# Third context attention: the filter's spectrum computed inside the self-attention in front of it

## The reference

```python
# self-attention of layer 2: two causal softmax attentions with 16 heads of 8, and their difference
q1, k1, q2, k2 = (x @ W for W in (Wq1, Wk1, Wq2, Wk2));  v = x @ Wv      # v: 16 heads of 16
a1, a2 = softmax(causal(q1 k1^T * scale)), softmax(causal(q2 k2^T * scale))
y = normalise_heads((a1 - lam * a2) @ v) * const;  x = x + y @ Wc

# context attention of layer 2: x -> top 32 of 1601 places per head (4 heads), then a long filter
dt = exp(log_dt);  dtA = dt * (A_re + 1j * A_im)            # 128 channels x 64 states
dC = (C_re + 1j * C_im) * (exp(dtA) - 1) / A
K  = 2 * einsum('dn,dnl->dl', dC, exp(dtA[:, :, None] * arange(256))).real
Kf = rfft(K, n=512)                                         # the filter's spectrum
y  = irfft(rfft(x, n=512) * Kf)[:256] + x * D_skip
```

## Time and profile before

| | us |
|---|---|
| median of 3 runs | 4265.91 |
| profiled execution, its own time | 4270.48 |
| span of the profiled execution, first to last instruction | 4268.6 |
| PE, DVE, ACT, POOL busy | 3312.7, 2984.5, 1868.6, 352.4 |
| `linear_columns`, second time (2503.7 to 2518.7) | 15.0 |
| first `self_attention` (2420.1 to 2503.7) | 83.6 |
| second `self_attention` (2518.7 to 2601.3) | 82.6 |
| first stage of `filter_spectrum` (2635.9 to 2701.2) | 65.3 |
| second stage of `filter_spectrum` (2701.2 to 2717.7) | 16.5 |

### The profile page before, as it was taken

The page is one execution under the profiler, slowest core; times in us unless marked ns, Lnnn a source line. Parts: engine busy times, 40 slices in busy tenths (PEclk is TensorE's granted clock), DMA queues, the critical chain, the costliest instruction groups (busy, mean ns, idle before and its releaser), DMA issues. The chain is left out here.

```text
span 4268.6 us, 58517 instructions
## 1 busy us (share of the span) xinstructions
PE 3312.7 (78%) x23817; PEld 1723.8 (40%) x23826; DVE 2984.5 (70%) x4070; ACT 1868.6 (44%) x2158; POOL 352.4 (8%) x150
## 2 busy tenths in 40 slices
PE   5799999999999965777776883466654669477579
PEld 3433333333333324344434652223222347344357
DVE  4577777777777776699996446699998444546642
ACT  2365565555555542344442233344443236245233
POOL 0000000000000000100000000044442000000000
PEclk9899999999999978799997997656567789688789
DMA  2000000000000000100002001000000100010010
GB/s 83 9 15 8 8 16 8 8 8 16 8 8 10 6 7 7 26 15 9 9 1 94 30 2 48 1 0 0 0 0 0 41 23 18 9 40 1 1 41 6
DMA packets 21598, 68.43 MB, mean 16 GB/s; under 512 B 5201, under 2 KB 5713, under 8 KB 20434
## 3 DMA queue, kind: packets, MB, share of 16 engines
q1 hardware_dynamic: 21330, 64.69, 5.1%
HBM read 49.07 MB, written 0.52 MB: 12 GB/s over the span
## 5 line engine op out<-in xcount | busy, mean ns | idle before, releaser
L1194 PE MATMUL banks<-L0x_ring,L0x_context_rows 128*101 128x512 f32 x1600 | 734.7, 602 | 4.0 <-ACT L0x_ring L1242 4.0
L1253 ACT COPY L0x_ring<-banks 128x1024 f32<-128x1024 f32 (+1 forms) x416 | 387.1, 982 | 536.4 <-PE banks L1182 536.4
L1182 PE MATMUL banks<-L0x_q_thirds,L0x_context_thirds 32*128 32x512 f32 x4800 | 596.2, 608 | 10.3 <-DVE L0x_q_thirds L1359 5.3
L1284 DVE TENSOR_TENSOR L0x_ring<-L0x_ring,L0x_greatest 128x2048 f32<-128x2048 f32 (+1 forms) x208 | 469.9, 2268 | 10.8 <-ACT L0x_ring L1253 9.4
L1300 DVE TENSOR_TENSOR L0x_maxima<-L0x_maxima,L0x_ring 128x1024 f32<-128x1024 f32 (+1 forms) x288 | 322.8, 1162 | 202.8 <-ACT L0x_ring L1253 202.7
L1194 PEld LDWEIGHTS banks<-L0x_ring,L0x_context_rows 128*101 128x101 f32 x1600 | 253.8, 167 | 456.0 <-issue 449.0
L1242 ACT ACTIVATE L0x_ring<-L0x_ring 128x2048 f32<-128x2048 f32 (+1 forms) x208 | 386.4, 1858 | 16.6 <-DVE L0x_ring L1284 16.2
L1182 PEld LDWEIGHTS banks<-L0x_q_thirds,L0x_context_thirds 32*128 32x128 f32 x4800 | 238.1, 186 | 348.5 <-issue 308.2
L1745 ACT ACTIVATE L1x_probs<-banks 128x2048 f32<-128x2048 f32 (+1 forms) x112 | 196.5, 1755 | 252.1 <-PE banks L1679 210.2
L1804 DVE TENSOR_REDUCE L1x_maxima<-banks 128x3 f32<-128x1203 f32 (+1 forms) x176 | 241.4, 1373 | 31.1 <-PE banks L1637 31.1
L1827 DVE SCALAR_TENSOR_TENSOR L1x_probs<-L1x_probs,L1x_floor 128x1024 f32<-128x1024 f32 (+1 forms) x208 | 252.1, 1216 | 11.3 <-ACT L1x_probs L1745 11.1
(11 more groups left out here) (954 smaller groups left out, 5227.2 us busy)
## 6 DMA issues: line engine op xcount, KB each, us to landing
L0x_q_thirds<-L0x_q_context SPq DMA_DIRECT2D x180, 64.0 KB, 2.0
L1f_expert_weights<-in_L1f_experts SPq DMA_DIRECT2D x16, 512.0 KB, 9.7
L2f_expert_weights<-in_L2f_experts SPq DMA_DIRECT2D x8, 512.0 KB, 6.0
L3a_expert_weights<-in_L3a_experts SPq DMA_DIRECT2D x8, 512.0 KB, 5.8
L3f_expert_weights<-in_L3f_experts SPq DMA_DIRECT2D x8, 512.0 KB, 6.5
L1x_k<-L1x_k_rows SPq DMA_DIRECT2D x64, 50.0 KB
L0x_context_thirds<-in_context_thirds SPq DMA_DIRECT2D x1, 2496.0 KB, 14.4
L1x_context<-in_context SPq DMA_DIRECT2D x4, 600.4 KB, 4.5
```

The source lines that it names most:

```text
L1182: mm = pe.matmul(k.ps[:, score_bank(s) + i, :], thirds[group_rows(i), slot, t, :], q_thirds[group_rows(i), u // 2 % 2, t, :], start=t == 0 ...
L1194: mm = pe.matmul(k.ps[0:CW, bank, :], rows1[0:height(j), j, :], ring[0:height(j), s % RING, i, :], start=s == FIRST[u] and i == 0, stop=s ...
L1253: act.copy(ring[0:r, s % RING, 2 * p:2 * p + len(pair), :], k.ps[0:r, bank:bank + len(pair), :]).then_inc(copied, 1)
L1284: dve.tensor_tensor(o, o, greatest[:, u % 2, None, :].broadcast_to([P, len(js), 512]), ALU.subtract).then_inc(shifted, 1)
```

## The change

The first stage of `filter_spectrum` is gone. Its work is spread over four places of layer 2's self-attention, in classes whose methods `linear_columns` and `self_attention` call (`beside`):

- `SpectrumRates`, in the first `linear_columns`: GpSimd computes `dt` and the rates, 29 instructions (12 two-input products, 14 with a scalar, on 128x128, and a memset and two iotas of 16).
- `SpectrumAngles`, in the first `self_attention`: GpSimd makes the multiples of the angle (2 products of 128x2048, with both inputs broadcast) and reduces two 128x128 angles (20 small instructions). DVE reduces the two 128x2048 angles, one or two instructions after `reduce(u+1)` in units 2 to 11. ACT takes all sines after its last unit.
- `SpectrumProducts`, in the second `self_attention`: GpSimd does 47 small instructions and 7 of 128x2048; ACT an exponential of 128x128 in unit 0, one of 128x2048 in unit 3 and one after the last unit; DVE a copy by mask and a reciprocal of 128x128 in unit 7.
- The loads of the spectrum's tables and of the context are issued in the last stage of the self-attention. The two masks are loaded in the stage that was the second of `filter_spectrum`, and ACT widens the context mask there, after its copies.

The working tiles lie where the context and the rows of the context attention lie later, and `best_places` keeps its exponentials where the tables were.

```diff
@@ self_attention
                     act.copy(yT[...], k.ps[:, 4:4 + n, spare]).then_inc(copied, 1)
+                    if beside:
+                        beside.scalar(act, u)
+                if beside:
+                    beside.after(act)
...
+                other = beside.vector(dve) if beside else iter(())
                 reduce(0)
                 for u in range(len(units)):
                     shift(u)
                     if u + 1 < len(units):
                         reduce(u + 1)
+                    next(other, None)
@@ new: the angles on DVE (SpectrumAngles.vector: two units nothing, then this twice)
+def turn_angle_by_turns(step, dve, angle, work, turns, radians, done):
     step(dve.tensor_scalar(work, angle, 1.0 / (2 * float(np.pi)), turns, ALU.mult, ALU.add))
+    step.start(dve.tensor_scalar(work, work, MAGIC, MAGIC, ALU.add, ALU.subtract))
+    yield
+    for c in RANGE:                                    # three constants
+        step.settle()
+        step.start(dve.scalar_tensor_tensor(out=angle, in0=work, scalar=-c, in1=angle, op0=ALU.mult, op1=ALU.add))
+        yield
+    step.settle()
+    step(dve.tensor_scalar(angle, angle, radians, 3.1415925, ALU.add, ALU.min))
+    dve.tensor_scalar(angle, angle, -3.1415925, None, ALU.max).then_inc(done, 1)
+    yield
@@ SpectrumAngles.after, on ACT behind the last unit
+        act.wait_ge(self.bent, 2)
+        act.activation(s2, s2, ACT.Sin).then_inc(self.sined, 1)
+        act.activation(x1, x1, ACT.Sin).then_inc(self.sined, 1)
+        act.wait_ge(self.turned, 1)
+        act.activation(a.high_part, a.high_part, ACT.Sin).then_inc(self.sined, 1)
+        act.wait_ge(self.turned, 2)
+        act.activation(a.low_part, a.sines, ACT.Abs).then_inc(self.sined, 1)
+        act.activation(a.sines, a.sines, ACT.Sin).then_inc(self.sined, 1)
+        act.wait_ge(self.sined, 5)
+        act.activation(a.low_part, a.low_part, ACT.Sin, scale=-1.0, bias=a.quarter).then_inc(self.sined, 1)
@@ SpectrumProducts.gpsimd, from the wait for DVE's unit 7 to the end
+        pool.wait_ge(self.chosen, 2)
...
+        step(pool.tensor_tensor(a.low_part, a.low_part, across(cA), ALU.mult))
+        step(pool.tensor_tensor(a.sines, a.sines, across(cB), ALU.mult))
+        step(pool.tensor_tensor(a.low_part, a.low_part, a.sines, ALU.add))
+        pool.wait_ge(self.exped, 2)
+        step(pool.tensor_tensor(a.low_part, a.low_part, a.decay, ALU.mult))
+        pool.tensor_tensor(a.decay, across(rate), along(a.sixteens), ALU.mult).then_inc(self.rated, 1)
+        pool.wait_ge(self.exped, 3)
+        step(pool.tensor_tensor(a.high_part, a.high_part, a.decay, ALU.mult))
@@ SpectrumProducts.after, on ACT behind the last unit
+        act.wait_ge(self.rated, 2)
+        act.activation(self.a.decay, self.a.decay, ACT.Exp).then_inc(self.exped, 1)
```

More of the change, by code:

```diff
@@ L387, in add_to_residual, with self_attention @@
     return write
-def self_attention(k, ctx_name, qT, kT, v, y, heads, dv, causal=True):
+def self_attention(k, ctx_name, qT, kT, v, y, heads, dv, causal=True, beside=None):
     groups = heads // 4
@@ L3729, in filter_spectrum @@
-def filter_spectrum(k, w, spectrum, c_all, hidden, mask, tiles):
-    full = [P, P, LOW]
-    with ExitStack() as ctx:
-        tables = k.sb("L2s_tables", [P, 2, HIGH // 4, FREQ], ctx=ctx)
-        small = k.sb("L2s_small", [P, 14, P], ctx=ctx)
-        angle, work, ev, U, V = (k.sb("L2s_" + n, full, ctx=ctx) for n in ("angle", "work", "e", "U", "V"))
-        t1, t2 = (tiles[:, 2 * i:2 * i + 2].rearrange("p a t n -> p (a t n)").rearrange("p (n l) -> p n l", l=LOW) for i in range(2))
-        power = k.sb("L2s_two_to_n", [P, P], I32, ctx=ctx)
+RANGE = (6.28125, 0.0019350051879882812, 2 * float(np.pi) - 6.28125 - 0.0019350051879882812)
@@ new lines, in across, with along, __init__, begin @@
+def across(row):
+    return row[:, :, None].broadcast_to([P, P, LOW])
+def along(row):
+    return row[:, None, :].broadcast_to([P, P, LOW])
+class SpectrumRates:
+    def __init__(self, a):
+        self.a = a
+    def begin(self, signal):
+        self.own = signal()
+    def gpsimd(self, pool):
+        a, w = self.a, self.a.w
+        dt, rate, th, em1, s2, nr, ni, wr, wi, mag, cA, cB, x1, x2, inv = a.small
+        pool.wait_ge(a.weights_here, 32)
+        step = Steps(pool, self.own)
+        step.start(pool.memset(a.quarter, float(np.pi / 2)))
+        step.start(pool.iota(a.ones, [[1, LOW]], base=0, channel_multiplier=0, allow_small_or_imprecise_dtypes=True))
+        step(pool.iota(a.sixteens, [[LOW, HIGH]], base=0, channel_multiplier=0, allow_small_or_imprecise_dtypes=True))
+        exponential_apart(step, pool, w["log_dt"], dt, mag, em1, a.power)
+        step.start(pool.tensor_tensor(th, dt, w["A_im"], ALU.mult))
+        step(pool.tensor_tensor(rate, dt, w["A_re"], ALU.mult))
@@ new lines, with __init__, begin, gpsimd @@
+class SpectrumAngles:
+    def __init__(self, a):
+        self.a = a
+    def begin(self, signal):
+        self.own, self.multiplied, self.by_dve, self.bent, self.turned, self.sined = (signal() for _ in range(6))
+    def gpsimd(self, pool):
+        a = self.a
+        dt, rate, th, em1, s2, nr, ni, wr, wi, mag, cA, cB, x1, x2, inv = a.small
+        step = Steps(pool, self.own)
+        pool.tensor_tensor(a.high_part, across(th), along(a.sixteens), ALU.mult).then_inc(self.multiplied, 1)
+        pool.tensor_tensor(a.sines, across(th), along(a.ones), ALU.mult).then_inc(self.multiplied, 1)
+        step(pool.tensor_scalar(s2, th, 0.5, None, ALU.mult))
+        turn_angle_apart(step, pool, s2, mag, em1).then_inc(self.bent, 1)
+        step(pool.tensor_copy(x1, th))
+        turn_angle_apart(step, pool, x1, mag, em1).then_inc(self.bent, 1)
+    def vector(self, dve):
+        a = self.a
+        step = Steps(dve, self.by_dve)
+        yield
+        yield
+        dve.wait_ge(self.multiplied, 1)
+        yield from turn_angle_by_turns(step, dve, a.high_part, a.decay, a.w["turns"], a.w["radians"], self.turned)
+        dve.wait_ge(self.multiplied, 2)
+        yield from turn_angle_by_turns(step, dve, a.sines, a.decay, 0.0, 0.0, self.turned)
+    def scalar(self, act, u):
+        pass
+    def after(self, act):
+        a = self.a
+        s2, x1 = a.small[4], a.small[12]
+        act.wait_ge(self.bent, 2)
[8 more added lines that the diff above has]
+        act.activation(a.low_part, a.low_part, ACT.Sin, scale=-1.0, bias=a.quarter).then_inc(self.sined, 1)
@@ L3742, in filter_spectrum @@
+def filter_spectrum(k, a, spectrum, hidden, mask):
+    U, V, tables = a.low_part, a.high_part, a.tables
+    with ExitStack() as ctx:
         kt = k.sb("L2s_filter", [P, HIGH // 4, P], ctx=ctx)
         seen = k.sb("L2x_mask_bytes", [1, B * CTX], U8, ctx=ctx)
-        quarter = k.sb("L2s_quarter_turn", [P, 2], ctx=ctx)
-        dt, a, th, em1, s2, nr, ni, wr, wi, mag, cA, cB, x1, x2 = (small[:, i, :] for i in range(14))
+        masked = k.sb("L2x_masked", [P, 1], ctx=ctx)
         with k.stage() as (block, signal):
-            here, masks, own, constants, rates, multiples = (signal() for _ in range(6))
-            bent, sined, exped, kept, absolute = (signal() for _ in range(5))
+            product, by_dve, by_act, spectral = signal(), signal(), signal(), signal()
+            masks, constants = signal(), signal()
@@ L3867, in filter_spectrum @@
-        with k.stage() as (block, signal):
-            product, by_dve, by_act, spectral = signal(), signal(), signal(), signal()
+                sp.dma_start(mask[:], k.dram["text_mask"]).then_inc(masks, 16)
+                sp.wait_ge(masks, 32)
+                sp.wait_ge(a.context_here, 16)
             def spread(i, r):
```

279 lines of the change are left out of this document (142 added, 137 removed).

## The result

The changed kernel takes 4215.1 us (median of 4 runs, 4211.97 to 4216.35), the kernel before 4268.3 (4 runs, 4263.62 to 4274.48) beside it: a ratio of 0.9872, 95% interval 0.9856 to 0.9888. That is 53 us; between the profiled executions 54.5 (4270.48 and 4216.03). Forecast were 60.0 us and 4206. The direction, the size and the range hold; of the forecast gain 5.5 us are missing between the profiled executions and 6.8 between the medians. The time itself lies 9.2 us above the forecast one: these 6.8, and 2.4 by which the kernel before was slower beside it than the 4265.91 on which the forecast stood.

The account below looks back on a forecast made before the run. The engine ending each stage was taken as the bound, VectorE in the removed one: 65.0 - 0.5 - 3.2 - 1.3 = 60.0 us off 4265.9, giving 4205.9; 8 in 10 range 4199 to 4224.

Parts of the forecast that it names:

- The stage removed, 65.0: First stage of filter_spectrum: taking it out lets TensorE begin the remaining filter stage 65.0 us sooner.
- Rates, nothing: First linear_columns: GpSimd's rates take 12.7 us in a stage of 15.2, so they cost nothing.
- VectorE between the units, 0.5: First attention: angle steps go into VectorE's 2.20 us idle per unit; 0.5 us for all ten units, bounds 0 and 1.8.
- Rival B: First attention: angle steps break the units' rhythm, every step adding its full length, giving 4229 us; chance 0.05.
- The sine tail, 3.2: End of first attention: ScalarE's table load and sines end at 2506.8, VectorE had ended at 2503.62; stage 3.2 us longer.
- The second attention, 1.3: GpSimd is ready 1.5 us in time; the last exponential and large product make the stage 1.3 us longer.
- Rivals A: GpSimd is late in the second attention, with broadcast inputs at half speed or dearer small steps: 4212 to 4226; chance 0.15.
- A2: Each run of 16 columns costs GpSimd a part of its own in large broadcast steps: 4226 to 4273; chance 0.04.
- Rival C: GpSimd and VectorE exclude each other altogether, in reduce and shift too; at all 86 us the time is 4292; chance 0.03.
- in the changed program this stage begins where the first began: Second filter stage: TensorE begins at 2636.48 instead of 2701.49, which is 65.0 us less.
- the 5.0: Time in us forecast to be added elsewhere than in the removed stage; 9.8 was measured.

Follow-up runs that it names:

- e_bare: Changed kernel without the filter spectrum's work beside the attention (GpSimd fills its two arrays with 0.5), a ceiling only: 4210.0 us.
- e_one_block: Changed kernel with VectorE's ten angle steps in one place, between units 2 and 3 of the first attention: 4239.2 us.
- e_load_later: Changed kernel with the load of the next feed-forward layer's weights issued two stages later: 4209.9 us.
- e_busy_one: Changed kernel with 13 more GpSimd products of 2048 columns, results unused, in the first attention beside VectorE's angle steps: 4237.3 us.
- e_in_lambda: Changed kernel with GpSimd's last product moved from the second attention's tail to the head of the head-statistics stage: 4212.4 us.
- e_load_more: Changed kernel with more data loaded behind the 1.4 MB ahead of the filter's stage; only 0.6 MB more came: 4213.7 us.
- e_four_more: Changed kernel with GpSimd computing the exponent of the last decay five times instead of once, in the second attention: 4225.0 us.
- e_load_rows: Changed kernel with the weight load two stages later and GpSimd's last product beside the last linear_rows: 4212.3 us.

## Why the prediction was right, and where it was short

**The stage removed, 65.0.** Right: in the new trace TensorE starts at once, and the sum of the stages has 65.01 less for it.

**Rates, nothing.** Right. GpSimd needed 13.1 us of the stage's 15.0, with 12.7 forecast.

**VectorE between the units, 0.5.** Nothing measurable, by e_bare. The cover was read rightly from the earlier trace rows: e_one_block shows that it is 2.2 us a unit and not a bit more. Rival B had the steps cost their full length spread out; they do so only in one block.

**The sine tail, 3.2.** 3.4 against e_bare, 2.7 to 3.4 behind VectorE's end in the traces with the same units. Right; what is not in the sum is the clock's part, up to 2.0 us on the attention and columns 2 together.

**The second attention, 1.3.** Between nothing and 1.4. At the same granted clock of 0.96 the stage is 83.6 to 84.3 us with the work and 84.13 without it. In e_load_later, at 0.98 as before, it was 1.4 longer than before, with GpSimd's product last by 0.6. GpSimd's price was too high: three of the five large steps behind its wait read broadcast inputs at 3.7 to 3.8 us instead of 4.52. It was ready 72.1 us into the stage, not 75.3, and had 5.2 us in hand and not 1.5. Two of the signs named ahead were wrong for this reason: its large steps do not all read 4.5 us, and the stage of after ends 0.1 us behind VectorE and not 1 to 2. Rivals A and A2 fall with that. The Trainium skill (GPSIMD Engine Reference, Performance pitfalls for Q7 kernels), by which each small read command would pay some 102 cycles, does not apply to runs of 16 in one instruction: such steps were the quicker ones (3.7 to 3.8 us against 4.52).

**Rival C, the engines exclude each other.** Its price of 86 us falls, since `reduce` and `shift` kept their lengths. Its mechanism is real. What avoided it is what stands beside what: `reduce` and `shift` read PSUM, and GpSimd was through with its work in the first attention after 20.9 us, when VectorE had done the angle steps of one unit of ten. After shows it in small, where GpSimd's reduction of the small angles meets VectorE's first two steps:

```profile
2436.37 1.62 POOL L3731 TENSOR_SCALAR L2x_contexts<-L2x_contexts 128x128 f32<-128x128 f32 x1
2436.57 1.28 DVE L3738 TENSOR_SCALAR L2x_contexts<-L2x_rows,L_weights 128x2048 f32<-128x2048 f32 x1
...
2438.07 1.35 POOL L3732 TENSOR_TENSOR L2x_contexts<-L2x_contexts 128x128 f32<-128x128 f32 x1
```

GpSimd's 0.53 and 0.46 became 1.62 and 1.35, and nobody waited for them. With large products in their place, e_busy_one paid 28 us. The Trainium skill (SBUF — State Buffer, Who interferes with whom) calls this an exclusive lock on the second pair of ports; e_busy_one and e_in_lambda agree, the latter with a step of 16 columns.

**What failed.** The step "in the changed program this stage begins where the first began" took the remaining stage over at its old length. I counted the loads that were moved, but not the one that was not: `use` issues 1.4 MB for the next layer, which lay 66 us ahead of TensorE's 256 small products, and with the stage between them gone lies 1.6 us ahead. TensorE's own instructions come behind it, by the packets' times some 2 us late. The stop is 1.0 to 1.8 us long, and the filter's stage got 2.6 to 3.2 longer than before in the ten kernels that have it. With the load moved the sum of the stages falls by 61.4 us, forecast 60.0, but 3.6 of the 5.2 gained in the filter are that trace's luck with the clock. So of the 4.8 us between the 9.8 and the 5.0 this step accounts for 3.0 in the trace of after. That the rest of the sum came out so near has some luck in it too: up to 1.8 us forecast for VectorE and GpSimd did not show, and the clock's part behind the tail and a slightly longer `linear_rows` took their place.

**What stays open.** Why the granted clock is low for 3.4 us near the border of the first attention and columns 2 even in e_bare, at another place than before, and why rows is up to 1.7 us longer than before (2.2 in e_load_more), e_bare included, at a lower granted clock in most. The moved work isn't the cause of these, as e_bare shows. Whether the changed program as a whole is, or whether the one trace of before was lucky there, can't be told from one trace of it.

## What to carry to other kernels

Work hides in a rhythm at the price of zero if each piece is about as long as the idle time of its engine in one round (pieces of 2.3 to 2.5 us in 2.2 here), and at nearly its full price if the same pieces stand together. Before a stage is taken out, look at what it kept apart: a large load that was far ahead of a burst of small instructions may then stand right in front of it, and delay, as far as the packets' times tell, not the data but the code. On GpSimd beside VectorE ask of each pair of steps whether both read and write SBUF; with VectorE reading PSUM they ran beside each other freely here (`reduce` and `shift` kept 1.81 and 0.41 us beside products of 3.8 to 5.7).

## What the hardware showed that I had not expected

- GpSimd's product of 128x2048 with a broadcast input takes 3.7 to 3.8 us, with plain inputs 4.52. Four in a row in e_four_more took 15.47 us, 3.87 from start to start, so it is no artefact of the recorded spans.
- On GpSimd a step with a scalar on 128x128 takes 0.30 us in some forms and 0.53 to 0.66 in others (L3765 and L3728 in the rows above).
- Instruction packets, TensorE's by their timing, queue with data: they come 2.0 to 2.6 us into the filter's stage without a load, 3.7 to 4.3 behind 1.4 MB, and a stop of 1.0 to 1.8 us in all ten kernels that had the load there.
- A stop of that length was followed in all ten by a granted clock of 0.50 and by 7.2 us for the 128 products that took 3.85 at full clock. A run without the stop (e_load_rows) had the low clock there as well, so the stop is not needed for it.
